# Turning the keys on VectorE and through DRAM, and SyncE's program written by steps

## What is computed

```
Q, K = x @ Wq.T, x @ Wk.T          # 16 heads of 64
V    = x @ Wv.T                     # 16 heads of 16
cg   = cumsum(-exp(A_log) * softplus(x @ Wdt.T + dt_bias))
Lam  = softplus(Lp * (x @ Wdl.T))   # 12 levels a head
W[t, s] = (Q[t] . K[s]) / 8 * exp(cg[t] - cg[s]) * Lam[t, level(t, s)]   for s <= t
o = layernorm(W @ V @ Wout.T + x);  x = layernorm(x + o)
```

## Time and profile before

| engine | busy us | share |
|---|---|---|
| TensorE, matmuls | 657.1 | 97% |
| TensorE, weight loads | 594.8 | 87% |
| VectorE | 486.8 | 72% |
| ScalarE | 337.0 | 50% |
| GpSimd | 353.9 | 52% |

### The profile page before, as it was taken

One profiled execution on the slowest core, in us unless ns is written; L12 is line 12 of the kernel. 1 busy time (PEld: TensorE's weight loads), 2 busy tenths in 40 slices (PEclk: granted clock), 3 DMA queues, 4 the chain that ended last, 5 costly groups with the idle time before them and its releaser, 6 DMA issues.

```text
span 680.5 us, 22147 instructions
## 1 busy us (share of the span) xinstructions
PE 657.1 (97%) x9114; PEld 594.8 (87%) x9114; DVE 486.8 (72%) x1100; ACT 337.0 (50%) x755; POOL 353.9 (52%) x475
## 2 busy tenths in 40 slices
PE   9989999999999999999999999999689999999994
PEld 7889999999999999899999999999588788888894
DVE  2864887879787978676797879787749565555556
ACT  4565454445545454545445454545253434555555
POOL 1716555646474655656464646556365435444435
PEclk9999999999999999999999999999888999999997
DMA  8122131312222141213132322313126503140002
GB/s 306 30 56 60 48 75 41 76 46 71 64 53 76 42 94 42 64 41 76 43 74 55 60 73 45 87 50 82 53 71 122 103 9 62 47 86 31 32 33 92
DMA packets 91987, 45.47 MB, mean 67 GB/s; under 512 B 39664, under 2 KB 90480, under 8 KB 91888
## 3 DMA queue, kind: packets, MB, share of 16 engines
q1 hardware_dynamic: 91888, 44.06, 25.6%
HBM read 34.60 MB, written 9.44 MB: 65 GB/s over the span
## 4 chain that ended last, share of the span: by engine, by line
PE 86%; DVE 5%; ACT 2%; POOL 2%; DMA 1%; SPq 1%; issue 1%; DVEq 0%; ACTq 0%; POOLq 0%
PE bank L437 64%; PE bank L461 5%; PE bank L528 5%; PE bank L440 5%; PE bank L493 4%; PE bank L557 4%; DMA xt<-in_wffn 1%; ACT t L791 1%; SPq L371 1%; DVE t L1028 1%; DVE t L1031 1%; POOL t L1415 1%; SPq L348 0%; POOL yL L1415 0%; DVE W L1028 0%
## 5 line engine op out<-in xcount | busy, mean ns | idle before, releaser
L437 PE MATMUL bank<-xH,wH 128*128 128x256 f32 x480 | 144.3, 301 | 1.2 <-ACT KT L791 0.9
L437 PE MATMUL bank<-xL,wH 128*128 128x256 f32 x480 | 135.0, 281 | 0.0
L437 PE MATMUL bank<-xH,wL 128*128 128x256 f32 x480 | 134.6, 280 | 0.0
L1028 DVE TENSOR_TENSOR W<-bank,E 128x512 f32<-128x512 f32 x128 | 82.0, 685 | 25.7 <-PE bank L437 25.4
L437 PEld LDWEIGHTS bank<-xH,wH 128*128 128x128 f32 x480 | 90.4, 188 | 7.8 <-issue 7.3
L437 PEld LDWEIGHTS bank<-xL,wH 128*128 128x128 f32 x480 | 90.5, 189 | 0.4
L437 PEld LDWEIGHTS bank<-xH,wL 128*128 128x128 f32 x480 | 90.5, 188 | 0.0
L791 ACT ACTIVATE E<-bank 128x512 f32<-128x512 f32 x128 | 66.1, 602 | 48.8 <-PE bank L461 48.8
L791 ACT ACTIVATE QT<-bank 128x512 f32<-128x512 f32 x64 | 38.2, 597 | 98.5 <-PE bank L437 98.5
L437 PE MATMUL bank<-QT,KT 64*128 64x128 f32 x1024 | 65.8, 278 | 0.0
L437 PEld LDWEIGHTS bank<-QT,KT 64*128 64x128 f32 x1024 | 59.6, 188 | 4.5 <-issue 0.5
(11 more groups left out here) (151 smaller groups left out, 1657.9 us busy)
## 6 DMA issues: line engine op xcount, KB each, us to landing
cB<-scr SPq DMA_DIRECT2D x240, 64.0 KB, 3.0
xt<-in_xT SPq DMA_DIRECT2D x16, 256.0 KB, 3.1
xs<-in_x SPq DMA_DIRECT2D x16, 256.0 KB, 3.1
xscr<-tx SPq DMA_DIRECT2D x32, 128.0 KB, 2.0
yT<-xscr SPq DMA_DIRECT2D x64, 64.0 KB, 2.4
out<-xs SPq DMA_DIRECT2D x16, 256.0 KB, 2.1
xt<-in_wffn SPq DMA_DIRECT2D x8, 256.0 KB, 3.1
QT<-in_wqk SPq DMA_DIRECT2D x4, 256.0 KB, 5.7
```

Source lines behind the costliest of these rows:

```text
L437: return e.matmul(o, a, b, start=start, stop=stop)
L1028: return e.tensor_tensor(o, a, b, op)
```

## The change

TensorE's keys and ScalarE's keys go, with the waits on their banks. In their place:

- VectorE turns KT in blocks of 32 x 32, a quarter (two of eight feature blocks, all 256 tokens, 128 x 512) at a time: turn_keys. The quarters of group sg are turned at the end of steps 8 sg - 7, 8 sg - 4, 8 sg - 3 and 8 sg (key_jobs), into kx, one buffer. For group 0 the four are turned at step -2 into W.
- SyncE stores each quarter in DRAM (kscr, 256 KB, rows of 2 KB): store_keys; kx is free for the next quarter when its store has landed.
- SyncE loads Kt for each chunk with four transfers of 32 partitions, 128 KB each, in runs of 32 elements: load_keys. For an even chunk 2 sg it is issued at step 8 sg, behind the landing of the fourth quarter's store; for an odd one at step 8 sg + 3; each behind the state product of the chunk before, which reads Kt.
- state waits for the landing of the four loads.

SyncE's program goes by steps instead of groups: stores, key stores, key loads and coefficient loads each at the step where their input is made, the slices of the recurrent layer at steps NG - 20 + i (i < 2) and NG - 17 + i, NG = 128. The sum x1 is written in place into xs, and tx has one buffer, which makes room for kx.

The diff, cut to its core:

```diff
+def key_jobs(s):
+    out = []
+    for d, q in ((7, 0), (4, 1), (3, 2), (0, 3)):
+        if (s + d) % 8 == 0 and 1 <= (s + d) // 8 < NSG:
+            out.append(((s + d) // 8, q))
+    return out
...
+        kscr = nc.dram_tensor("kscr", (4 * NSG, 32, 2048), F32, kind="Internal").ap()
...
-        x1 = sb("x1", [P, 256])
-        tx = [sb(f"tx{i}", [P, 256]) for i in range(2)]
+        tx = sb("tx", [P, 256])
+        kx = sb("kx", [P, 512])
...
+            def store_keys(sg, q):
+                e.wait_ge(d_kx, 4 * sg + q + 1)
+                src, done = (kx[:, :], l_kx) if sg else (W[:, 4 * q:4 * q + 4, :].rearrange("p h t -> p (h t)"), l_k0)
+                e.dma_start(kscr[4 * sg:4 * sg + 4, :, 512 * q:512 * q + 512].rearrange("i t c -> (i t) c"),
+                            src).then_inc(done, 16)
+
+            def load_keys(ci):
+                sg, c = ci // 2, ci % 2
+                e.wait_ge(l_kx, 64 * sg) if sg else e.wait_ge(l_k0, 64)
+                if STATE[ci]:
+                    e.wait_ge(p_st, STATE[ci])
+                for j in range(4):
+                    b = 128 * c + 32 * j
+                    e.dma_start(Kt[32 * j:32 * j + 32, :].rearrange("t (q i f) -> t q i f", q=8, i=4),
+                                kscr[4 * sg:4 * sg + 4, :, :].rearrange("i t (q b) -> t q i b", q=8)[:, :, :, b:b + 32]
+                                ).then_inc(l_Kt, 16)
...
-            for sg in range(NSG):
-                if sg == NSG - 1:
-                    for i in range(2, 7):
-                        load_wf(i)
-                load_coefs(sg)
...
+            for s in STEPS:
+                for i in [i for i in range(8) if s == (NG - 20 if i < 2 else NG - 17 + i)]:
+                    load_wf(i)
+                for sg, j in token_jobs(s):
+                    if j == 5:
+                        store_coefs(sg)
+                if (sg := split_x_at(s)) is not None and sg + 2 < NSG:
+                    e.wait_ge(g_xl, sg)
+                    load_xt(sg + 2)
+                if (ci := chunk_at(s, 11)) is not None:
+                    store_turned(ci)
+                for q in range(4) if s == -2 else ():
+                    store_keys(0, q)
+                for sg, q in key_jobs(s):
+                    store_keys(sg, q)
+                if 0 <= s < NG and s % 8 == 3 and s // 4 + 1 in STATE:
+                    load_keys(s // 4 + 1)
+                if 0 < s < NG and s % 8 == 0 or s == -1:
+                    load_keys(max(s, 0) // 4)
+                for sg, j in token_jobs(s):
+                    if j == 5:
+                        load_coefs(sg)
+                        if sg + 2 < NSG:
+                            load_x(sg + 2)
+                if s in (NG - 8, NG - 7):
+                    load_turned(0, s - NG + 8)
+                if s in (NG - 2, NG + 5):
+                    for t in range(2):
+                        load_turned(1 if s < NG else 2, t)
...
-            def keys(ci):
-                c, b = ci % 2, (ci // 2) % 2
-                if c == 0:
-                    e.wait_ge(a_qk, 8 * (ci // 2) + 8)
-                for n in range(2):
...
-                e.wait_ge(m_free[km], ku + 1)
-                km, ku = MISC["keys", ci, 1]
-                e.wait_ge(m_free[km], ku + 1)
+                e.wait_ge(l_Kt, 64 * (STATE[ci] + 1))
...
+                if sg >= 2 and j == 1:
+                    e.wait_ge(d_kx, 4 * (sg - 2) + 4)
...
+            def turn_keys(sg, q):
+                e.wait_ge(a_qk, 8 * sg + 2 * q + 2)
+                src = KT[sg % 2][:, 2 * q:2 * q + 2, :].rearrange("p m t -> p (m t)")
+                if sg == 0:
+                    o = W[:, 4 * q:4 * q + 4, :].rearrange("p h t -> p (h t)")
+                else:
+                    o = kx[:, :]
+                    if sg > 1 or q:
+                        e.wait_ge(l_kx, 16 * (4 * (sg - 1) + q))
+                e.transpose(o, src).then_inc(d_kx, 1)
...
                 if (ci := chunk_at(s, 11)) is not None:
                     outer_norm(ci)
                     turn_result(ci)
+                for sg, q in key_jobs(s):
+                    turn_keys(sg, q)
```

More of the change, by code:

```diff
@@ L85, in misc_jobs @@
         ci, cc = s // 4, (s // 4) % CB
-        if s % 4 == 0 and cc < CB - 1:
-            out += [("keys", ci, 0), ("keys", ci, 1)]
         if s % 4 == 1 and cc:
@@ L325, in load_wf @@
             def load_wf(i):
-                if i >= 2:
+                if i < 2:
+                    e.wait_ge(g_xl, NSG - 2 + i)
+                else:
                     e.wait_ge(g_wf, i - 1)
@@ L329, in load_wf, with store_coefs @@
                     l_xt[i % 2], 16)
-            def load_coefs(sg):
+            def store_coefs(sg):
                 m, u = MISC["cft", sg, 0]
@@ L352, in store_turned @@
                 e.wait_ge(d_tx, ci + 1)
-                e.dma_start(xscr[4 * ci:4 * ci + 4, :, :].rearrange("i f c -> (i f) c"), tx[ci % 2][:, :]).then_inc(
-                    l_tx[ci % 2], 16)
+                e.dma_start(xscr[4 * ci:4 * ci + 4, :, :].rearrange("i f c -> (i f) c"), tx[:, :]).then_inc(l_tx, 16)
+            def store_keys(sg, q):
[13 more added lines that the diff above has]
+                                ).then_inc(l_Kt, 16)
             def load_turned(blk, t):
                 c0 = 16 * t + 4 * blk
-                for i in range(2):
-                    e.wait_ge(l_tx[i], 16 * (c0 // 2 + 2))
+                e.wait_ge(l_tx, 16 * (c0 + 4))
                 if blk == 0:
@@ L392, in _ @@
             load_xt(2)
-            for sg in range(NSG):
-                if sg == NSG - 1:
-                    for i in range(2, 7):
-                        load_wf(i)
-                load_coefs(sg)
[L398 to L414, removed]
-                    store_turned(ci)
+            store_coefs(0)
+            load_coefs(0)
+            e.wait_ge(g_xl, 1)
+            load_xt(3)
+            load_x(2)
+            for s in STEPS:
[8 more added lines that the diff above has]
+                if (ci := chunk_at(s, 11)) is not None:
+                    store_turned(ci)
+                for q in range(4) if s == -2 else ():
[16 more added lines that the diff above has]
+                        load_turned(1 if s < NG else 2, t)
@@ L752, in _ @@
                 if 0 <= ci < NC:
-                    if n == 0 and ci in STATE:
-                        keys(ci)
                     if n == 1:
@@ L878, in exps @@
                     act(E[:, :, 32 * q:32 * q + 32], XP[q][:, :].rearrange("p (h t) -> p h t", h=H), ACT.Exp).then_inc(a_e, 1)
[L880 to L886, removed]
             def split_ffn(i):
@@ L990, in _ @@
                     act(c0H[:, :, :], bc(c0, 2, 2), ACT.Copy).then_inc(a_c0, 1)
-                if 0 <= s < NG and s % 4 == 0 and s // 4 in STATE:
-                    keys(s // 4)
                 for sg, j in project_jobs(s):
@@ L1060, in weights @@
                 e.wait_ge(a_e, 4 * ci + 4)
+                if ci == 0:
+                    e.wait_ge(l_k0, 64)
                 if ci:
@@ L1361, in _ @@
             for s in STEPS:
+                if s == -2:
+                    for q in range(4):
+                        turn_keys(0, q)
                 if (ci := chunk_at(s, 5)) is not None:
```

27 lines of the change are left out of this document (13 added, 14 removed).

## The result

The changed kernel takes 767.22 us (median of four runs, 763.41 to 773.26) against 682.35 for the kernel before, run beside it: a ratio of 1.126, 95% interval 1.117 to 1.134. It is slower by 85 us. The forecast was 704, its range 660 to 734, so the sign was right and the time lies 33 us above the range.

A forecast was written before the change was run, and what follows sets the result against it. TensorE was taken to bound the chunk loop, busy all 32.00 us of a pair. From 682.1: -29.6 transposes, +40.5 key waits, +4 CT, -6.8 loop end, +14 clock = +22, forecast 704 us, range 660 to 734.

The forecast's parts named there:

- Transposes, -29.6: TensorE loses eight products a chunk, 1.02 us each chunk, counted as 29.6 us saved.
- Waits for keys, 40.5: TensorE waits 2.7 us for Kt before the state product in each of 15 even chunks, 40.5 us.
- Rival 4: SyncE late from its 16 loads, or store landing in 4.1: 1.9 us more each wait, 748 us; chance 0.10.
- TensorE's arrival, +12.5: TensorE reaches the even state product 12.5 us after the even chunk's exponents start, without its transposes.
- Waits on VectorE, +4: Quarter 2's turn ahead of CT delays the next even chunk 0.3 us a pair, 4 us in 14 pairs.
- End of the loop, -6.8: At the loop's end, a 9.8 us stall and cold restart goes, about 3 us remain, net -6.8.
- The clock, +14: Clock falls after waits for keys, about 2 us each, 30 in all 15; half taken, +14 us.
- Rival 2: Same waits for keys, and each brings the clock down: 720 us; chance 0.10.
- Rival 3: Key transfers land near their shortest, path nearly hidden, wait 1.0 us: faster, 664 us, or 650 without wait; chance 0.26.
- Rival 5: Transfers hidden but VectorE becomes the bound in the chunk loop, 31.1 us a pair: 670 us; chance 0.04.

The follow-up runs named there:

- run 2: Run 1 with VectorE's 64 turns added at the changed kernel's places, written into kx and read by nobody: 688.57 us, ratio 1.007.
- run 1: Changed kernel with TensorE and ScalarE turning the keys as before; SyncE's program by steps, sum in xs and single tx stay: 672.73 us, ratio 0.986.
- run 4: Changed kernel with 44 unused matmuls ahead of the wait for Kt in even chunks 2 to 28: 751.72 us, ratio 1.101.
- run 5: Changed kernel with the turn and store of the last key quarter one step earlier: 762.27 us, ratio 1.117.
- run 9: Changed kernel, keys projected first in blocks 2 to 14, second half of cB loads behind the stores of the next block's first two quarters: 695.62 us, ratio 1.016.
- run 6: Run 5 with the second half of the cB loads issued behind the even chunk's key loads: 705.19 us, ratio 1.032.

## Why the prediction was wrong

The mechanism was the one forecast: removed products, a path that ends later than TensorE, a clock that falls in the wait. Three terms of the sum were too small: the waits for keys, the waits on VectorE and the clock.

- **Transposes, -29.6.** The 240 products are gone, at 1.02 a chunk; no run contradicts the term, and none measures it by itself.
- **Waits for keys, 40.5; measured 61.7.** The pattern was right (even chunks only, the odd load hidden), but chunk 0 waits too, 3.9 us where I had counted 1. The path was put at +15.2 and ended at +17.45 in the mean of the 13 pairs, and every part of it was short: turn 7.4, measured 7.8; gap to the store 0 ("free by then, but barely"), measured 0.4; store to first load 2.2, measured 2.9; first load to product 5.6, measured 6.3. The two landings are 1.4 of the 2.25 that are missing, the queue ahead of the store 0.4. The queue becomes the bound only when the turn is moved forward: an earlier turn alone gained 5 us, with SyncE freed as well 62. Rival 4 named both causes, SyncE late or a slow store, and had 0.10 and 1.9 us more in each wait; measured is 1.1 more. It is closest to what happened, though its 748 is still 19 short. The earlier trace rows were no good measure of SyncE either: their 8.07 is the shortest of the thirteen groups of 16 cB loads in that trace, whose median is 8.9.
- **TensorE's arrival, +12.5.** Measured: state at 17.45 less a mean wait of 3.79 in the 13 pairs, +13.7. Run 2 has the cause of more than half of it, +13.2: VectorE's turns hold TensorE back in many small places. The rest is open.
- **Waits on VectorE, +4; by run 2 +15.8.** I had looked at the two places where a turn stands ahead of a known row with a small margin. S, yt, zt and zs, each late by 1.0 us at most, were not in the sum; in run 2 the waits for S alone are 7.3 us.
- **End of the loop, -6.8; by run 1 -9.6.** The standstill of the earlier trace rows went with its cold restart, as forecast. In the changed kernel the gain is covered: chunks 28 and 30 wait 3.8 and 4.7 for their keys there, and the 16 loads of yT are issued behind them.
- **The clock, +14, half of 15 waits at 2 us.** It fell during or just behind every one of the 13 waits; the three ways of run 4 give 34 to 38 us in the 13 pairs, 2.6 to 2.9 each. Both halves of the term were low, the share (1, not 0.5) and the price. The price came from 4.3 us at half the clock after the standstill; behind the waits TensorE was busy at half the clock for 5.9 us in the mean (76.3 / 13).

With the measured terms: -29.6 + 61.7 + 15.8 - 9.6 = +38.3. The two profiled executions are 91.2 apart, so 52.9 are left. Half of the time that TensorE was busy at 1.2 GHz is 51.7 us in the whole changed kernel and 3.4 in run 1, whose end the sum has: the clock accounts for some 48 of the 52.9. About 5 us may be the traffic or VectorE again; no run separates them. Against the medians, 84.9 apart, the same terms come out about 1 us high.

Rival 2, every wait brings the clock down, was right in its mechanism; I gave it 0.10 since the rows had one fall only. The Trainium skill (TensorE: Matmul & The Clock Gate, "HAM oscillation") describes a loop that waits for a DMA in every pass and starts each pass cold, and this trace agrees, with 12 of 13 pairs at 2.09; the waits of that loop are 3 to 5 us, near the 2.8 to 5.3 measured here and longer than the 2.7 of my forecast.

The trace of the kernel before has a second fall, which I overlooked, and it came without a wait. TensorE had no gap from 510.82 on, but the 36 matmuls just before the state product had two columns each (windows, then the timeline):

```profile
518.24:522.40 4.16, 4.16 (x38) 4.13 (x36) 3.99 (x9) 0.00 (x0) 0.00 (x0) 1.00 0.68 154
522.40:524.10 1.70, 1.70 (x33) 1.68 (x33) 1.60 (x7) 1.35 (x3) 0.64 (x1) 0.57 0.78 146
```

```profile
522.26 0.25 PE L437 MATMUL bank<-c0H,wL 128*128 128x2 f32 x1
522.44 1.76 PE L557 MATMUL bank<-Vw,Kt 128*64 128x16 f32 x32
524.13 2.09 PE L461 MATMUL bank<-CT,AT 32*128 32x128 f32 x32
```

The changed kernel has the same fall at its end (at 602.5, among the same 36 matmuls), so not every fall there is due to the keys.

Rival 3 (landings near their shortest) is refuted: the kscr stores landed in 3.4 in the median and the Kt loads in 3.8:

```profile
Kt<-kscr SPq DMA_DIRECT2D x120, 128.0 KB, 3.8
kscr<-kx SPq DMA_DIRECT2D x60, 256.0 KB, 3.4
```

The Trainium skill (DMA: Bandwidth & Descriptors, "Anatomy of one DMA") fits 2.0 us and the bytes over 436 GB/s to DMAs that GpSimd issues, which these are not; an estimate by it is 2.3 for such a load. The row has 3.8, and the row decides. Rival 5 (the transfers hidden, VectorE the bound) is refuted by the waits for keys, and by run 2, where TensorE is busy for 411.4 of 420.5 us.

The range failed because the misses did not vary one by one: a wait in every pass brought the fall of the clock with it in every pass, and VectorE's delays, a miss of their own, pointed the same way. I had let each be near its middle.

## What to carry to other kernels

When a step moves from a full engine to a path of transfers, write down the moment at which the issuing queue is free as well as the one at which the data is ready, and move both: here an earlier turn alone was worth 5 us, and with eight loads in another order 62. In the changed kernel itself the queue cost only 0.4 us a pair. Read a duration from all its occurrences, not from the one pair at hand. A wait that recurs in each pass is to be priced at its length plus the slow stretch behind it, here 3.8 plus 2.6 to 2.9 us; and a single buffer between two queues lets a late issue in one hold up the other. Test the parts of a change alone: one half of this one was a gain of 1.4% under a net loss of 12.6%.

## What the runs showed of the hardware that I had not expected

- A load of 1024 runs of 128 B keeps SyncE's queue for 0.68 us in the median (four in 3.01), a load of cB for 0.43. The keys' traffic did not slow the issue of the cB loads in the changed kernel: sixteen cB loads took 8.1 to 9.9 us before, median 8.9, and 8.6 to 9.6 in the changed kernel, median 8.8.
- Single issues are sometimes long: one store of tx of 32 took 2.04 us (299.99 in the changed kernel), where most take 0.3 to 0.5. Run 1, without the keys' traffic, has one of 1.8.
- Waits of the same length did not act alike. The first row is of the changed kernel, at 1.2 GHz, and its exponents took 2.09; the second is of run 5, at the full clock behind the same wait, and its exponents took 1.17:

```profile
196.96 1.90 PE L583 MATMUL bank<-Vw,Kt 128*64 128x16 f32 x32 [2.84 <-issue]
193.38 1.11 PE L583 MATMUL bank<-Vw,Kt 128*64 128x16 f32 x32 [2.84 <-issue]
```

- In run 9 waits for CT of 1.48 and 1.49 were followed by exponents of 1.17 at 117.59 and 149.87, and one of 1.49 by 2.09 at 215.79; in run 6 waits for keys of 1.51, 2.13 and 2.52 were followed by 2.04 to 2.09, one of 1.31 by 1.58, those of 0.95, 1.02 and 1.20 by 1.17, and one of 0.33, with 1.09 more for CT behind the product, by 1.77.
- The clock also fell without a wait, behind 36 matmuls of two columns each, as shown above for the kernel before; all eleven traces have a fall among these 36 or within 1.3 us of their end.
- Useless matmuls in place of a wait made the kernel faster: 767.22 to 746.62.
